# Folding the second layer norm into the up-weights and the spike thresholds

## The reference

```
x  = x + context(layernorm(x)) @ wo.T      # q, k, v of width 64; energy = k.T v per batch; context = q energy * sqrt(3/64)
x  = x + spikes(W_proj @ relu(W_fc @ layernorm(x))**2) / 5
layernorm(x) = (x - mean) / sqrt(var + 1e-5)
spikes(y): mem = 0.9 mem + y - [mem > 1], five steps, counts how often the new mem > 1
```

## Time and profile before

| | |
|---|---|
| median of 3 runs | 515.51 us (513.12 to 517.15) |
| profiled execution: span from the first to the last instruction | 509.8 us |
| mean granted TensorE clock, share of full speed | 0.983 |
| busy PE, PEld, DVE, ACT, POOL | 484.9, 437.2, 359.8, 284.7, 208.7 us |
| chain that ended last | PE 89%, DVE 6%, issue 2%, DMA 1% |

### The profile page before, as it was taken

How to read it: one execution, slowest core, us unless ns; L and a number is a source line. 1 busy time by engine, 2 the same in 40 slices (tenths; PEclk the granted TensorE clock), 3 DMA queues, 4 the chain that set the end, 5 groups by cost and what they waited for, 6 DMA issues and landing times.

```text
span 509.8 us, 9252 instructions
## 1 busy us (share of the span) xinstructions
PE 484.9 (95%) x3092; PEld 437.2 (86%) x3092; DVE 359.8 (71%) x991; ACT 284.7 (56%) x519; POOL 208.7 (41%) x171
## 2 busy tenths in 40 slices
PE   6798899999999989999999979999999999999995
PEld 5577789999989879898999969999998989999995
DVE  5876748777777656776887765778777764939447
ACT  2445846556665626657556544655666575656540
POOL 2434533443434414344344423444343443445440
PEclk9979999999999989999999999999999999999998
DMA  7110101111101011010111100111100101010102
GB/s 294 66 42 0 43 0 43 42 44 42 42 0 65 22 45 42 1 70 15 42 42 42 42 18 30 43 42 42 42 1 0 42 2 42 0 42 2 42 1 82
DMA packets 5810, 19.93 MB, mean 39 GB/s; under 512 B 640, under 2 KB 1280, under 8 KB 5504
## 3 DMA queue, kind: packets, MB, share of 16 engines
q1 hardware_dynamic: 5760, 19.27, 10.1%
HBM read 10.88 MB, written 8.39 MB: 38 GB/s over the span
## 4 chain that ended last, share of the span: by engine, by line
PE 89%; DVE 6%; issue 2%; DMA 1%; ACT 0%; SPq 0%; POOL 0%
PE hid_ps L707 12%; PE y_ps L709 11%; PE y_ps L708 11%; PE y_ps L707 11%; PE hid_ps L709 11%; PE hid_ps L708 11%; PE work_ps L747 3%; PE work_ps L732 2%; PE work_ps L816 2%; PE work_ps L817 2%; PE work_ps L707 2%; PE work_ps L708 1%; PE work_ps L709 1%; DVE cnt L626 1%; PE e_ps L797 1%
## 5 line engine op out<-in xcount | busy, mean ns | idle before, releaser
L312 POOL TENSOR_TENSOR hid_l<-hid,hid_h 128x512 fp32r<-128x512 f32 x128 | 165.9, 1302 | 253.8 <-ACT hid_h L364 253.7
L353 ACT ACTIVATE relu<-hid_ps 128x512 f32<-128x512 f32 x128 | 76.7, 599 | 128.6 <-PE hid_ps L709 128.5
L709 PE MATMUL y_ps<-wdn_h,hid_l 128*128 128x256 f32 x480 | 136.3, 284 | 0.0
L708 PE MATMUL y_ps<-wdn_l,hid_h 128*128 128x256 f32 x480 | 136.1, 284 | 0.0
L707 PE MATMUL y_ps<-wdn_h,hid_h 128*128 128x256 f32 x480 | 135.7, 283 | 0.0
L707 PE MATMUL hid_ps<-x2T_h,wup_h 128*128 128x512 f32 x256 | 106.3, 415 | 6.8 <-issue 6.5
L709 PE MATMUL hid_ps<-x2T_h,wup_l 128*128 128x512 f32 x256 | 100.5, 392 | 0.0
L708 PE MATMUL hid_ps<-x2T_l,wup_h 128*128 128x512 f32 x256 | 100.4, 392 | 0.0
L708 PEld LDWEIGHTS y_ps<-wdn_l,hid_h 128*128 128x128 f32 x480 | 91.9, 191 | 4.9
L707 PEld LDWEIGHTS y_ps<-wdn_h,hid_h 128*128 128x128 f32 x480 | 91.8, 191 | 5.0
L709 PEld LDWEIGHTS y_ps<-wdn_h,hid_l 128*128 128x128 f32 x480 | 91.9, 191 | 0.0
(11 more groups left out here) (106 smaller groups left out, 633.7 us busy)
## 6 DMA issues: line engine op xcount, KB each, us to landing
xs<-x_dram SPq DMA_DIRECT2D x15, 512.0 KB, 3.4
out_dram<-x SPq DMA_DIRECT2D x15, 512.0 KB, 3.1
hid<-w_up_dram SPq DMA_DIRECT2D x1, 1024.0 KB, 7.9
x<-w_down_dram SPq DMA_DIRECT2D x1, 1024.0 KB, 10.0
xs<-x_dram SPq DMA_DIRECT2D x2, 256.0 KB, 2.9
out_dram<-x SPq DMA_DIRECT2D x1, 256.0 KB, 2.0
out_dram<-x SPq DMA_DIRECT2D x2, 128.0 KB, 1.9
wkv_raw<-w_kv_dram SPq DMA_DIRECT2D x1, 128.0 KB, 3.3
```

Of the source, the lines that this page charges most:

```text
L312: nc.gpsimd.tensor_tensor(hid_l[:, i % 2, c, :], hid[:, c % 4, :], hid_h[:, i % 2, c, :].bitcast(f32), ALU.subtract).then_inc(hid_ready, 1)
L353: nc.scalar.activation(relu[:, c % 2, :], hid_ps[c % 2][:, :], ACT.Relu).then_inc(relu_done, 1)
L708: mm(dst, a[0], b[1], start=False, stop=False)
L709: return mm(dst, a[1], b[0], start=False, stop=stop)
```

## The change

The second norm is no longer applied to x1. Its mean is taken out of the up-weights on the chip: a 128 x 128 matrix of 1/256 times the up-weights gives the mean over the 256 rows for each column, and DVE subtracts it from the raw weights. The product of centred weights and raw x1 equals that of the weights and centred x1. The inverse deviation r is a positive factor per token; relu, square and down-projection carry it to r squared, so y > THETA becomes y' > THETA (var + eps). x1 is turned as it is; DVE makes the 20 bounds of each token and group with one small product, and the comparisons take their threshold from it instead of from the instruction.

```diff
+            nc.gpsimd.memset(averager[:, :], 1.0 / EMB).then_inc(averager_ready, 1)
+            for level in range(NUM_STEPS):
+                nc.gpsimd.memset(theta[:, level:level + 1], THETA[level]).then_inc(theta_ready, 1)
             pool.wait_ge(ident_zero, 1)
...
             low_half_of_weights(wdn_high, wdn_raw, wdn_h, wdn_l, wdn_ready, 0)     # POOL
-            inverse_deviation(0, 0, 1)
             low_half_of_weights(wdn_high, wdn_raw, wdn_h, wdn_l, wdn_ready, 1)
...
-                    if c == 4 and there(r, i + 1):                                 # POOL, each step
-                        inverse_deviation(r, i + 1, 1)
...
             xnT_high_half(0, 1)                                                    # ACT
-            half_of_columns(w_loaded["up"], wup_raw, wup_h, wup_high, 0)
+            half_of_columns(wup_centred, 2, wup_raw, wup_h, wup_high, 0)
             kvT_out(0, 0)
             kv_high_half(0, 0)
             kvT_out(0, 1)
             q_high_half(0, 0)
             kv_high_half(0, 1)
-            half_of_columns(w_loaded["up"], wup_raw, wup_h, wup_high, 1)
+            half_of_columns(wup_centred, 4, wup_raw, wup_h, wup_high, 1)
...
+            def centre_weights(k):                                                 # DVE
+                rows = wup_raw.rearrange("p (k n) -> p k n", k=EC)[:, k, :]
+                for h in range(2):
+                    cols = slice(h * HID // 2, (h + 1) * HID // 2)
+                    dve.wait_ge(wup_mean, h + 1)
+                    nc.vector.tensor_tensor(rows[:, cols], rows[:, cols], (y_ps[1], e_ps)[h][:, :], ALU.subtract)\
+                        .then_inc(wup_centred, 1)
+            def bounds(r, n):
+                dve.wait_ge(moments_ready[1], upto(r, n + 1))
+                nc.vector.tensor_tensor(bound[:, n % RING, :, :], <theta, broadcast over 4 tiles>,
+                                        <ve[1], broadcast over 5 levels>, ALU.mult).then_inc(bound_ready, 1)
...
-                        nc.vector.scalar_tensor_tensor(acc, y, THETA[level], acc, ALU.is_gt, ALU.add)\
+                        nc.vector.scalar_tensor_tensor(acc, y, over, acc, ALU.is_gt, ALU.add)\
...
                 if there(r, i - 1):                                                # DVE, each step
                     spikes(r, i - 1, 0, range(0, PAIR_OPS // 2))
                 if there(r, i + 1):
-                    normalise(r, i + 1, 1)
+                    bounds(r, i + 1)
...
             low_half_of_weights(wqq_high, wqq_raw[:, :], wqq_h, wqq_l, wqq_ready)  # DVE, prologue
+            centre_weights(0)
+            centre_weights(1)
             first_moments(0, 2)
             kv_low_half(0, 0)
             normalise(0, 2)
...
             residual(0, 0)
+            x2T_low_half(0, 0)
             moments(0, 0, 1)
+            bounds(0, 0)
             q_low_half(0, 2)
-            normalise(0, 0, 1)
             kv_low_half(0, 2)
-            x2T_low_half(0, 0)
             first_moments(0, 3)
...
+            def mean_of_weights(h):                                                # PE
+                cols = slice(h * HID // 2, (h + 1) * HID // 2)
+                pe.wait_ge(averager_ready, 1)
+                pe.wait_ge(w_loaded["up"], 16)
+                rows = wup_raw.rearrange("p (k n) -> p k n", k=EC)
+                for k in range(EC):
+                    last = mm((y_ps[1], e_ps)[h][:, :], averager[:, :], rows[:, k, cols], start=(k == 0), stop=(k == EC - 1))
+                last.then_inc(wup_mean, 1)
...
+                pe.wait_ge(x1_ready, upto(r, n + 1))                               # turn_second
                 for t in range(TILES):
-                    if t % 2 == 0:
-                        pe.wait_ge(norm_ready[1], upto(r, n, 2, t // 2 + 1))
...
             project_kv(0, 0)                                                       # PE, prologue
+            mean_of_weights(0)
             project_kv(0, 1)
+            mean_of_weights(1)
             turn_kv(0, 0)
             project_q(0, 0)
             turn_kv(0, 1)
+            pe.wait_ge(wup_centred, 4)
             energy_sum(0, 0)
...
             project_kv(0, 2)
             project_q(0, 2)
+            turn_second(0, 0)
             turn_kv(0, 2)
-            keep_warm(3)
-            turn_second(0, 0)
+            keep_warm(3, work_ps[1])
             energy_sum(0, 2)
-            keep_warm(3, work_ps[1])
             steps(pe, step)
```

More of the change, by code:

```diff
@@ L94, in build @@
         ident = sb("ident", [P, P])
+        averager = sb("averager", [P, P])
         xs = sb("xs", [P, RING, GE])
@@ L123, in build @@
         neg_half = sb("neg_half", [P, TILES])
+        theta = sb("theta", [P, NUM_STEPS])
+        bound = sb("bound", [P, RING, TILES, NUM_STEPS])
         hid_ps = [bank(f"hid_ps{n}") for n in range(2)]
@@ L339, in high_half_of_weights, with half_of_columns @@
                 nc.scalar.activation(high[:, :, :], raw, ACT.Copy).then_inc(out_high, 1)
-            def half_of_columns(loaded, raw, high, out_high, h):
-                act.wait_ge(loaded, 16)
+            def half_of_columns(loaded, count, raw, high, out_high, h):
+                act.wait_ge(loaded, count)
                 chunks = slice(h * high.shape[1] // 2, (h + 1) * high.shape[1] // 2)
@@ L461, in _ @@
             xnT_high_half(0, 2)
-            half_of_columns(w_loaded["down"], wdn_raw, wdn_h, wdn_high, 0)
+            half_of_columns(w_loaded["down"], 16, wdn_raw, wdn_h, wdn_high, 0)
             kvT_out(0, 2)
@@ L465, in _ @@
             kv_high_half(0, 2)
-            half_of_columns(w_loaded["down"], wdn_raw, wdn_h, wdn_high, 1)
+            half_of_columns(w_loaded["down"], 16, wdn_raw, wdn_h, wdn_high, 1)
             x2T_high_half(0, 0)
@@ L513, in moments, with normalise @@
                     .then_inc(moments_ready[which], 1)
-            def normalise(r, n, which):
-                b = lane(r, n, which)
-                dve.wait_ge(rstd_ready[which], upto(r, n + 1))
-                if there(r, n - 1) and b == which:
-                    dve.wait_ge(norm_turned[which], upto(r, n))
-                if isinstance(r, int) and which == 1 and n == 0:
-                    dve.wait_ge(norm_turned[0], 2)
+            def normalise(r, n):
+                b = lane(r, n, 0)
+                dve.wait_ge(rstd_ready, upto(r, n + 1))
+                if there(r, n - 1) and b == 0:
+                    dve.wait_ge(turned[0], upto(r, n))
                 for t in range(TILES):
                     cols = slice(t * EMB, (t + 1) * EMB)
-                    last = nc.vector.tensor_scalar((xn, x2n)[b][:, cols], (xs, x1)[which][:, n % RING, cols],
+                    last = nc.vector.tensor_scalar((xn, xn_1)[b][:, cols], xs[:, n % RING, cols],
                                                    mv[b][:, t, 0:1], rstd[b][:, t:t + 1],
@@ L529, in normalise @@
                     if t % 2:
-                        last.then_inc(norm_ready[which], 1)
+                        last.then_inc(norm_ready, 1)
             def residual(r, n):
@@ L603, in spikes @@
                         dve.wait_ge(y_free, upto(r, n, 2, pair + 3))
+                    if level < NUM_STEPS:
+                        over = bound[:, n % RING, 2 * pair + a, level:level + 1]
                     if level == 0:
-                        nc.vector.tensor_scalar(acc, y, THETA[0], None, ALU.is_gt).then_inc(count_step, 1)
+                        nc.vector.tensor_scalar(acc, y, over, None, ALU.is_gt).then_inc(count_step, 1)
                     elif level < NUM_STEPS:
-                        nc.vector.scalar_tensor_tensor(acc, y, THETA[level], acc, ALU.is_gt, ALU.add)\
+                        nc.vector.scalar_tensor_tensor(acc, y, over, acc, ALU.is_gt, ALU.add)\
                             .then_inc(y_free if o == PAIR_OPS - 3 else count_step, 1)
@@ L646, in step @@
                 if there(r, i + 3) and not is_first(r, i):
-                    normalise(r, i + 3, 0)
+                    normalise(r, i + 3)
                 if there(r, i + 2) and closes_batch(i + 2):
@@ L675, in _ @@
             first_moments(0, 1)
-            normalise(0, 0, 0)
-            normalise(0, 1, 0)
+            normalise(0, 0)
+            normalise(0, 1)
             xnT_low_half(0, 0)
```

68 lines of the change are left out of this document (41 added, 27 removed).

## The result

| | time, us (runs) | before beside it, us (runs) | ratio, 95% |
|---|---|---|---|
| changed kernel | 522.18 (521.26 to 527.35, 4) | 515.34 (513.12 to 517.15, 4) | 1.0195 [1.0138, 1.0251] |

It is slower by 6.8 us, and 522.6 was forecast. The interval leaves no doubt that it is slower, but not whether by more or less than 2%. One execution of one kernel further down (e7) took 969.8 us, nearly twice its others, and is left out of every number here.

The account below looks back on a forecast made before the run. PE was taken to bound the loop, leaving only the prologue to change: +7.0 + 1.2 - 1.1 = +7.1 on a span of 509.8 gives 516.9, with 5.7 added 522.6 us; range 516.5 to 526.5.

Parts of the forecast that it names:

- first half, to the residual: Prologue: means on PE and subtractions on DVE delay everything behind on DVE, residual of group 0 at 38.9: +7.0 us.
- residual to first up: Prologue, residual of group 0 to first up-projection: x1's normalisation goes, but the kv copy is late next: +1.2 us.
- step 0: First step: PE's two waits for x1's normalisation go: -1.1 us.
- steps 1 to 14: Loop: DVE's savings and added costs stay hidden under PE, whose waits stay unchanged: 0.
- from step 15 on: Behind the last matmul: 20 comparisons with thresholds from memory stand on the path; 0 to +1.0 us, taken as 0.
- rival A: Prologue: wup_h's second copy comes after normalise(0, 2), PE may keep its clock: +2.7, 518.2, not slower; chance 0.22.
- Clock: 0: Prologue: half-clock stretch behind PE's 3.7 us pause stays, as a pause of the same kind stays: 0.
- The threshold: DVE's comparisons: threshold from memory costs 0, by L526; from above 0.05 us for each operand.
- The 5.7 us: Whole kernel: amount by which the median stands above the profiled span, added to 516.9 to give 522.6.
- B: Loop: the four issue pauses (6.5 us) and their slow stretches close and rival A holds: 510, faster; chance 0.07.
- C: Loop: threshold from memory uses up DVE's slack; at +0.5 us an instruction 35 us, 558; chance 0.03.
- D: Prologue: the means fall in a slow stretch of PE's clock: +3.5, 526.1; chance 0.08.

Follow-up runs that it names:

- e7: The changed kernel with all steps written out, no loop on any engine: 510.35 us (3 runs), ratio 0.9900.
- e6: The kernel before with all steps written out, no loop on any engine: 501.37 us, ratio 0.9746.
- e1: The changed kernel with the five thresholds as constants in the comparisons again, bounds still made: 521.79 us, ratio 1.0176.
- e4: The changed kernel with four idle transposes ahead of the first turning: 515.39 us, ratio 1.0038.
- e11: e7 with e8's reordering, and group 3's statistics and norm ahead of x1's moments, its deviation ahead of the last wdn_l on POOL: 503.82 us, ratio 0.9775.
- e2: The kernel before with only the centring of the up-weights added, second norm still applied: 509.58 us, ratio 0.9919.
- e8: The changed kernel with group 2's q and k, v low halves ahead on DVE, x1's high half ahead of the down-weights on ACT: 521.17 us, ratio 1.0146.
- e3: The kernel before with four idle transposes ahead of the first turning: 514.56 us, ratio 1.0013.
- e5: The kernel before with eight idle transposes ahead of the first turning: 505.43 us, ratio 0.9804.
- e10: e6 with ACT's up-weight high halves behind the first batch's k, v copies, second down-weights part behind x1's high half: 494.54 us, ratio 0.9620.
- e12: e11 with the centring moved behind the first batch's energy and ACT's weight copies behind the chain: 502.81 us, ratio 0.9768.

## Why the prediction came out right, and where it was wrong

The time was inside the range and on the forecast's side, but by luck: the terms were off by up to 6.5 us, in both directions. Its steps stand against two pairs: the profiled ones, and the unrolled ones (e6, e7), in which the loop turns have no part.

| step | forecast | before to after | e6 to e7 |
|---|---|---|---|
| first half, to the residual | +7.0 | +0.5 | +7.4 |
| residual to first up | +1.2 | +1.9 | +1.4 |
| step 0 | -1.1 | +0.8 | +0.15 |
| steps 1 to 14 | 0 | +4.7 | 0.0 |
| from step 15 on | 0 (bound +1.0) | +1.8 | +1.8 |
| sum, span | +7.1 | +9.6 | +10.7 |

*First half: right in mechanism, and both of its outcomes occur.* e7 has `normalise` at 5.46 us beside both wup_l and the residual 7.4 us later than e6, 1.0 of it because its first projection started that much later (14.43 against 13.47); e1, e4 and e11 meet both copies too. After's own profiled execution, e2 and e8 missed the collision (3.42 us each): rival A, given 0.22. There the residual moved by 0.5 us only. The statistics are 5.2 us later and not 7.0, mostly because in this execution PE was free for the means at 14.13 instead of 15.80. The missed copy took 2.1 (3.0 are left at the low half of k and v of group 1, 27.44 against 24.46), and PE's work up to the residual at full clock took 2.4 more, 5.0 us against 7.4.

The outcomes form two groups. In e1, e4, e7 and e11 the second wup_h ends 1.9 us behind the start of `normalise`, as forecast, with PE at full clock in the turns ahead of it; in after, e2 and e8 it ends 3.3 to 3.5 us behind, with a stretch at half clock there (22.5 to 25.9 us in after). That is the slip of 1.5 us "from ACT or a slow clock in the turns" that rival A asked for. Why the clock falls there in some executions and not in others stays open.

*Residual to step 0: right.* The copy of k and v was late next, with PE's wait of 5.8 us for it, in all versions that keep the order; e8 moved the copies and took 5.4 us of it away.

*Step 0: the waits went, the clock did not stay.* The two waits for the normalised x1 (1.1 us) are gone. But "Clock: 0" looked at the first pause only. PE's longer pause ahead of the energy is followed by a start at half clock: 15 matmuls in after's first 5.5 us, against 25 in before's at a clock of 1.00. The runs that keep after's order share this out. Step 0 took 17.65, 17.86, 18.75 and 18.98 us in e4, e1, after and e7, at a mean granted clock of 0.93, 0.92, 0.87 and 0.85. Less the share that the clock took, each has 16.1 to 16.4 us left, and e11, which stayed at 1.00, took 16.41. So of after's +0.8, -1.7 are the waits and +2.4 the clock, by this estimate. In e7 against e6 the same -1.7 stands against a clock of 0.85 where e6 had 0.95, which leaves +0.15.

*The loop's work: right; the loop's turn: the missed term.* DVE and POOL kept their slack, and e7 equals e6 to 0.01 us. What grew is the pause that the forecast had read in the earlier trace rows, put down to PE's issue, and left unchanged except in a rival that made it shorter. It depends on where the loop lies in the program: +4.7 us here. e3 makes it of four idle transposes, e2 and e5 take it away, e6 has none. Only the first half, at 6.5 us, was off by more in the profiled pair, and that outcome stood among the rivals; a longer pause at the turn stood nowhere.

*The threshold: mis-sized.* 0 was taken, by L526, which reads two such operands in 0.40 us; the upper bound, 50 ns, was nearly the truth (60 ns). It is felt only at the end, but on 30 instructions, not 20: the last pair of the group ahead pushes the start of the last 20.

*Around the span.* The 5.7 us were no time around the span; that is 1.9. They were mostly the distance of before's median from a quick execution. The sum of the steps was 2.5 us short (+7.1 against +9.6): terms of +4.7 and +1.8, which it lacked, and 2.6 more between the residual and step 1 stand against a first half that was 6.5 us cheaper in the profiled execution. The 5.7 us then added 3.8 too much. That 522.6 and the median of 522.18 lie so close is these errors cancelling; the unrolled pair, without the turns, has +7.4, +1.4 and +0.15 where +7.0, +1.2 and -1.1 were forecast.

*The rivals.* A came true up to the residual, and its 518.2 was missed by what the turn, step 0 and the end added. B did not: in after no pause closed. But its premise holds, that the pauses depend on more than PE's work: in e4, the same change behind four idle transposes, PE's own pause is gone. "Nothing in the change shortens PE's loop" looked at the work and not at the place. C did not occur, as no wait for DVE appeared, though its sign did: the mean of the comparisons in the loop is 0.474 us, above the 0.46 that was named. At +62 ns each, 20 of them use 1.2 us of a step's slack of 9.5. D, means in a slow stretch, did not occur: 0.47 us per instruction. The trace spoke less clearly against D than the forecast said. The clock read 1.00 from 4.5 to 11.0 us, but also from 7.1 to 10.1 with PE idle, and 0.50 from 11.2 to 14.6.

The Trainium skill (SBUF — State Buffer, Who interferes with whom) says that when DVE works in a two-port mode beside GpSimd, whichever issues first keeps the shared ports for its whole instruction, and the other is blocked. The runs agree: `normalise` of four instructions took 1.38 us with no copy beside it, 3.42 with one of 2.37, and 5.46 with two, so each copy adds about 2.0, most of its length.

Open is how PE's instructions are fetched. The 30 packets for 0.49 MB in the profile's page are 16.3 KB each, and a pause that moves with four and eight idle transposes, and goes together with 18 packets of the queue, fits a loop that, by its place in such blocks, has to be fetched again at each turn or not; this was inferred, not shown. Open is also what makes executions of one kernel differ by up to 7.5 us, the collision in the prologue being one part of it that the traces do show (first up-projection 44.9 or 48.9).

## What to carry to other kernels

Before you believe a difference of 1 or 2% in a kernel with a loop, write the loop out or shift it by a few idle instructions: here the same loop cost 2.6 to 13.7 us by its place, about as much as the change under study. See at such a turn which engine stands: DVE stood 2.5 us too, and was felt only where PE did not. Sort the prologue by who is waited for first: the weight copies, needed last, stood ahead of the chain on ACT and made DVE's `normalise` four times as long through POOL, and moving them was worth 7 us (e6 to e10), while the change cost 9.0 (e6 to e7). When a copy is moved, look in the step behind for what it meets there: e8 and e12 gave back 3 and 8 us.

## What the runs showed of the hardware

- PE's own pause at a loop turn: 1.5 + 2.4 us from start to start (before) or 4.9 (after, e3), with up to 6.8 us of half clock behind it; none in e2, e4 and e5, where the same loop lies at another place, and none when written out. Steps 1 to 14, with the same work in PE, took 400.3 to 414.6 us; of that range 413.3 to 414.6 (e1, after, e8) have the loop at one and the same place in PE's program.
- DVE's own pause at a loop turn: 2.5 to 2.8 us in every kernel with a loop, none without. PE felt it only in e2, e4 and e5, as a wait of 1.1 to 1.9 us.
- 30 packets in the instruction queue q8 with PE's pause, 12 without it, 24 with the loop written out.
- A threshold from memory in DVE's comparisons: 484 against 424 ns on the last tiles, 474 against 412 in the loop. `normalise`, which reads two operands of that kind per instruction, was no guide to it.
- The small product `bounds` took 0.17 us mostly and 0.57 at most; the stall behind POOL that was feared for it hardly came (mean 219 ns), as 13 of its 16 instructions met no POOL instruction at all; the two at the end that met a copy early took the 0.57. The residual of the counts, with both inputs in SBUF, took longer than before, 589 against 451 ns in the mean, hidden in DVE's slack: steps 1 to 14 are equal in e6 and e7.
